# A graph layer on one core: positions written out, counts in fixed chunks, rows kept resident, nine dense tiles

## The chip, the cores and the metric

The kernel runs on one core of a Trainium2 chip. The metric is the device time of one execution in microseconds (us); a time "before" is the median of three runs. Engine names in the rows: PE is the matrix engine (PEld its weight loads), DVE the vector engine, ACT the scalar engine, POOL GpSimd, SP the engine that here only starts transfers and passes on their arrivals. A "q" behind a name (DVEq) is that engine's sequencer.

## The reference

```python
xn = layernorm(x)                                  # x is 6250 x 256, float32
h = maxk(xn @ W_neigh, 32)                         # each row keeps its 32 largest values
summed = segment_sum(h[src], dst)                  # 200000 edges, dst is sorted
neigh = summed / max(degree(dst), 1)
mix = ((q(xn) @ context) * gate(xn)) @ Wproj + bproj   # context: softmax(k) over all rows, times v
x = x + xn @ W_self + neigh + mix
y = layernorm(x)
w = y @ wr + br                                    # 3124 rows with the largest w are selected
out = x + y, and for the selected rows: + (gelu(y @ w1 + b1) @ w2 + b2) * w
```

What matters here is `summed`. The targets are drawn as 6250 times the square of a uniform number, so the first targets have by far the most edges. Every row of h is kept as two float16 halves of 256 values, so a stored row is 512 float16 values (1 KB) in `rows_d` in the chip's memory.

## The kernel before

The 6250 rows are 50 tiles of T = 125. The edges, in the order of their targets, are cut into chunks of 128 and groups of four chunks (512 edges).

Three stages follow each other. The first (to about 330 us) lays out the edges, computes h and k and v for all tiles, stores the rows of h and forms the context. The second, which is what the change touches, is a row of 50 positions, one tile each: it sums the messages of the tile and computes everything up to w. The third selects rows and runs the feed-forward part.

A tile of the second stage is summed in one of two ways.

- A sparse tile is gathered. POOL issues four indirect DMAs for a group (`gathers`, L729), each bringing 128 rows of 1 KB into a ring of 8 groups; it may refill a slot when PE has counted up `s_slot_free`. DVE makes one-hot rows of the group's targets (`visit`, L1480, four chunks in one instruction), into a ring of 8. PE does four matmuls of 512 columns (L1074) and four of 2 columns for the degrees (L1075) per visit. A tile has one visit more than it has groups, because a group on a tile's edge is visited by both.
- A dense tile (the first tiles, with the most edges) is not gathered. Its sum is a matrix of counts (target row by source row) times all rows of h. The counts are made in 13 windows of 10 target rows. For each chunk of 128 edges of a window DVE makes a one-hot of the source's place in its tile (125 wide) and one of the combined key of target and source tile (500 wide), and PE multiplies them into a bank of PSUM (L1048). ACT copies a finished window to `counts16` (L866). When all 13 are there, PE multiplies the counts by the rows of h (L1117, 50 matmuls of 512 columns) and sums the degrees (L1123).

Eight tiles are dense. The 50 positions are three hardware loops (one turn of ten positions, three turns, one turn), and the order inside a turn is fixed by tables: `SHARE` says how many windows of the coming dense tile are counted at each sparse position, `SUMMED` at which positions the eight pieces of rows (`PIECES`, reloaded from `rows_d` by ACT for every dense tile into the two halves of `hs`) are multiplied. How many chunks a window has is found from the edges while the kernel runs: DVE and PE read the window's bounds with `value_load` (L459) and loop over pairs of chunks (`keys_of` on DVE, L1499 and L1507; `count` on PE, L1048). The pairs pass through a ring of 8 pairs, guarded by `s_hot` (DVE to PE) and `s_hot_free` (PE to DVE). A position's groups are cut into up to four stretches, and the windows are counted between them.

The order of the work in position n:

- PE: wait for `s_pfree` (DVE has read the projection of n-1); load the bounds of the coming position and the windows (L459); mix_hidden for n+2 (L1015), project for n (L1032, L1035), mix_open for n+1 (L1021, L1027); possibly one piece of rows; then the opening zero matmuls (L1142, L1143); visits, windows and pieces in turn; the closing matmuls (L1152, L1153), the last of which raises `s_agg`.
- DVE: one-hots of the visits and the keys of the windows in turn; `row_chain` of position n-1 (L1542 to L1570); base_x and base_p (L1606, L1609, which raises `s_pfree`); gate_pre for n+2 (L1467); mix for n+2 (L1471); the loads of bounds for the next position; wait for `s_agg`; copy the sum out (L1616 to L1621, raising `s_deg` and `s_aggfree`).
- ACT: the small transfers of the position, the tanh of the gate, the copies of finished windows, the reloads of `hs`, the GELU, and the store of the row block.
- SP: waits for every group's landing and passes it on as `s_landed`; after every four groups it starts a transfer of the next indices (`indices`, L595), without which POOL cannot go on.

## Time and profile before

| | us |
|---|---|
| median of three runs | 2484.12 (2483.62 to 2513.19) |
| the profiled execution: its own time | 2499.61 |
| its span (first to last instruction) | 2497.5 |
| clock granted to PE, mean over the span | 0.749 of full speed |
| PE busy | 1546.7 |
| DVE busy | 1280.0 |
| POOL busy | 1129.9 |
| ACT busy | 238.0 |

The span is what the rows below are read against; the execution's own time has 2.1 us more, and stands 0.6% above the median of the runs. Busy times of the engines overlap, and none reaches two thirds of the span.

### The profile page before, as it was taken

What the parts mean: (1) busy time and instruction counts of PE and PEld (TensorE: products, weight loads), DVE (VectorE), ACT (ScalarE), POOL (GpSimd) and SP (SyncE); (2) the same over time, 40 slices, a digit from 0 to 9 for tenths busy, and PEclk for the clock granted to TensorE, in tenths of its full rate; (3) what the DMA queues carried; (4) which work ended last, traced back from release to release, by engine and by line L of the source; (5) the groups of instructions that cost most, each with busy time, mean ns of one, the idle gap of its engine ahead of it and who ended that gap; (6) DMA issues with size and microseconds to landing.
All of it is one profiled execution on the core that took longest, in us unless ns stands there. A gap on an engine that the chain in (4) does not pass through costs nothing.

```text
span 2497.5 us, 35631 instructions
## 1 busy us (share of the span) xinstructions
PE 1546.7 (62%) x7023; PEld 1006.7 (40%) x7024; DVE 1280.0 (51%) x4041; ACT 238.0 (10%) x499; POOL 1129.9 (45%) x1207
## 2 busy tenths in 40 slices
PE   1985546565646655655665565646656756662998
PEld 0542433343333433433343343434433534442566
DVE  6999436554632366356346445446355365365111
ACT  1542200000000000000000000000000000000211
POOL 1455634566656445345533543624425255431312
PEclk8997667686767677767677767867766766875999
DMA  8221422233346322722632542722723733740301
GB/s 166 67 77 54 122 63 64 85 99 93 97 119 168 99 66 83 186 62 84 163 94 71 150 113 69 183 78 73 193 58 95 161 93 98 189 98 26 87 17 27
DMA packets 175766, 249.12 MB, mean 100 GB/s; under 512 B 39962, under 2 KB 135759, under 8 KB 175650
## 3 DMA queue, kind: packets, MB, share of 16 engines
q0 software_dynamic: 55152, 135.74, 20.0%
q10 hardware_dynamic: 90492, 91.90, 14.5%
q1 hardware_dynamic: 30006, 20.05, 3.5%
q8 instruction: 59, 0.97, 0.2%
q14 instruction: 57, 0.47, 0.1%
HBM read 211.32 MB, written 35.71 MB: 99 GB/s over the span
## 4 chain that ended last, share of the span: by engine, by line
PE 29%; issue 26%; DVE 15%; DVEq 9%; another core or an unknown queue 9%; DMA 8%; ACTq 2%; SPq 1%; POOL 0%; ACT 0%; POOLq 0%
PE bank L1074 6%; PE bank L1048 6%; DMA region_k<-rows_d 5%; PE bank L1193 3%; PE bank L1207 3%; DVE region_k L1507 2%; PE bank L1117 2%; DVEq L459 2%; PE bank L1032 2%; DVEq L1518 2%; DMA gs_wide<-gs_d 2%; DVE region_r L1381 1%; PE bank L1035 1%; DMA region_k<-in_x_dram 1%
## 5 line engine op out<-in xcount | busy, mean ns | idle before, releaser
L729 POOL DMA_INDIRECT ring<-rows_d,stage x960 | 948.1, 988 | 1018.6 <-PE bank L1074 661.9
L1074 PE MATMUL bank<-ring,region_v 128*125 x1120 | 418.9, 478 | 119.1 <-issue 113.9
L1048 PE MATMUL bank<-region_k 128*125 x830 | 292.6, 461 | 171.9 <-issue 147.8
L1507 DVE TENSOR_SCALAR region_k<-iota,win_start,region_k 128x500 f16 x830 | 306.3, 408 | 26.2 <-issue 21.7
L1480 DVE SCALAR_TENSOR_TENSOR region_v<-iota,tile_start,dstT 128x500 f16 x280 | 206.1, 739 | 181.1 <-issue 156.0
L1074 PEld LDWEIGHTS bank<-ring,region_v 128*125 x1120 | 178.1, 159 | 250.7 <-issue 195.8
L1499 DVE SCALAR_TENSOR_TENSOR region_k<-iota,region_k 128x250 f16 x415 | 173.2, 417 | 167.5 <-issue 110.7
L1616 DVE TENSOR_SCALAR col_deg<-bank 125x1 f32<-125x1 f32 x50 | 7.8, 157 | 469.7 <-remote 216.7
L1048 PEld LDWEIGHTS bank<-region_k 128*125 x830 | 115.5, 153 | 298.3 <-issue 282.8
L1015 PE MATMUL bank<-region_v,wg1g 128*64 128x125 f32 x208 | 51.9, 395 | 282.2 <-issue 262.3
L1075 PE MATMUL bank<-ones,region_v 128*125 128x2 f16 x1120 | 200.0, 179 | 7.5 <-issue 7.2
L1075 PEld LDWEIGHTS bank<-ones,region_v 128*125 x1120 | 182.5, 163 | 18.7 <-issue 16.9
L1117 PE MATMUL bank<-region_k 125*125 125x512 f16 x400 | 127.8, 467 | 90.9 <-DMA region_k<-rows_d 76.4
L1015 PEld LDWEIGHTS bank<-region_v,wg1g 128*64 128x64 f32 x208 | 33.7, 201 | 286.4 <-issue 283.1
L866 ACT ACTIVATE region_k<-bank 125x500 f16<-125x500 f32 (+1 forms) x104 | 60.1, 579 | 896.2 <-remote 532.6
L1117 PEld LDWEIGHTS bank<-region_k 125*125 125x125 f16 x400 | 60.4, 164 | 132.6 <-DMA region_k<-rows_d 83.8
L1032 PE MATMUL bank<-region_v 128*125 128x256 f32 x200 | 93.0, 609 | 5.6 <-issue 5.6
L960 PE MATMUL bank<-region_r 128*125 128x512 f32 x200 | 96.3, 604 | 0.0
L1193 PE MATMUL bank<-region_k,region_v 128*128 128x500 f32 (+1 forms) x224 | 88.2, 553 | 1.4 <-DVE region_k L1733 1.4
L1207 PE MATMUL bank<-region_v,region_k 128*125 128x256 f32 x400 | 87.3, 379 | 0.0
L753 POOL DMA_INDIRECT out_dram<-region_r,region_v x24 | 28.6, 1191 | 126.8 <-DVE region_r L1753 123.1
L1035 PE MATMUL bank<-region_v 128*125 128x256 f32 x200 | 79.6, 535 | 7.9 <-issue 7.9
(302 smaller groups left out, 1987.1 us busy)
## 6 DMA issues: line engine op xcount, KB each, us to landing
region_k<-rows_d ACTq DMA_DIRECT2D x48, 672.0 KB
ring<-rows_d,stage POOLq DMA_INDIRECT x960
kept_d<-region_v ACTq DMA_DIRECT2D x50, 252.0 KB
region_k<-rows_d ACTq DMA_DIRECT2D x16, 784.0 KB
region_v<-xT_d ACTq DMA_DIRECT2D x53, 125.0 KB
xT_d<-region_r ACTq DMA_DIRECT2D x51, 125.0 KB, 2.0
rows_d<-region_r SPq DMA_DIRECT2D x50, 125.0 KB
region_k<-in_x_dram ACTq DMA_DIRECT2D x50, 125.0 KB
```

Of the source, the lines that this page charges most:

```text
L729: pool.indirect_dma_start(out=ring[:, c, :], out_offset=None, in_=rows_d, in_offset=bass.IndirectOffsetOnAxis(ap=stage[:, c:c + 1], axis=0 ...
L1032: pe.matmul(p_sum, xTc[:, turn, k * T:(k + 1) * T], w_self[:, k, :], start=(k == 0), stop=False)
L1035: m = pe.matmul(p_sum, mixT[:, k, :], wproj[:, k, :], start=False, stop=(k == KC - 1))
L1048: m = pe.matmul(out, lo, key, start=False, stop=False, skip_group_check=True)
L1074: m = pe.matmul(total, onehot_s, row_s, start=False, stop=False, skip_group_check=True)
L1075: d = pe.matmul(deg_sum, onehot_s, ones16[:], start=False, stop=False, skip_group_check=True)
L1117: m = pe.matmul(dense_sum, counts16[:, b, :], hs[:, q % 2, (b - first) * 2 * C:(b - first + 1) * 2 * C], start=False, stop=False, skip_gro ...
L1193: m = pe.matmul(up_bank(n)[:, 0:wide], w1[:, k, n * 128:(n + 1) * 128], x3T[:, g % 2, k, 0:wide], start=(k == 0), stop=(k == KC - 1))
L1207: m = pe.matmul(y_pair(h)[:, u % 2, :], hid[:, g % 2, n, u * T:(u + 1) * T], w2[:, n, :], start=(n == 0), stop=(n == NH - 1))
L1480: dve.scalar_tensor_tensor(out=part(hot_bytes, HOT, SLOT_HOT, hot, 0, SLOT_HOT).bitcast(F16).rearrange("p (a t) -> p a t", a=GC), in0=iota ...
L1499: dve.scalar_tensor_tensor(out=part(pair_bytes, HOT_PAIRS, SLOT_PAIR, slot, 0, KEYS_AT).bitcast(F16) .rearrange("p (a t) -> p a t", a=PAIR ...
L1507: last = dve.tensor_scalar(part(pair_bytes, HOT_PAIRS, SLOT_PAIR, slot, KEYS_AT + u * KEYS * 2, KEYS * 2).bitcast(F16), iota[:, 0:KEYS], p ...
```

## The change

The change does eight things in the second stage.

1. The three hardware loops go. The 50 positions are written out, from a list `ORDER` made while the kernel is built.
2. Nine tiles are dense instead of eight.
3. A window has a fixed number of chunks, from the distribution of the targets (`window_chunks`: mean plus six roots of the mean, plus the share of a chunk that an unaligned start needs). The sum over the 117 windows is 978 chunks. If a window's edges didn't fit, the general path (everything gathered) would be taken.
4. The windows are cut into 126 units of at most 16 chunks. ACT loads a window's first chunk (one `value_load` for each window) and copies the source places and the keys of a unit to a small buffer at a fixed place, adding the window's start on the way (`stage`). DVE makes two one-hots for a chunk with two `tensor_scalar` instructions at fixed addresses; the ring holds 16 chunks, and PE frees it chunk by chunk. PE's count is one matmul for a chunk; the zero matmuls around a window go (the first and last matmul carry start and stop).
5. In a position, PE does all groups in one stretch, closes the sum and raises `s_agg`, and only then counts the position's units. DVE makes the one-hots of all visits, then `row_chain` of n-1, then the units' keys, then base_x and the rest as before.
6. All rows of h (6.4 MB) are loaded once by SP into `table`, after the context is done; a dense tile is then 50 pairs of matmuls (512 columns and 2 columns) at its own position. The reloads of `hs` and the pieces go.
7. DVE and PE load bounds only for the groups of sparse tiles.
8. In the first stage POOL fills the tables with some 110 small iotas and memsets instead of about ten, and DVE's short chain that makes the bounds is changed in a few steps.

By the build-time list, the sparse tiles 9 to 16 come first with 267 chunks counted beside them, then dense tile 0; then four sparse positions before each of the dense tiles 1 to 4, three before 5, four before 6 and 7, three before 8; the last three sparse tiles have no counts.

```diff
-    TURNS_OF = (1, 3, 1)
-    DENSE_AT = (9, 4, 6)
-    PAIR = 2
-    HOT_PAIRS = 8
-    SHARE = ((2, 2, 2, 2, 2, 2, 1, 0, 0, 0), (4, 4, 5, 0, 0), (4, 3, 3, 3, 0, 0, 0, 0, 0, 0))
+    ND = 9
+    COUNT_HOT = 16
+    UNIT = 16
+    STAGED = 8
+    def window_chunks(w):
+        low, high = (w // NW * T + min(w % NW * WIN + wide, T) for wide in (0, WIN))
+        mean = E * (math.sqrt(high / N) - math.sqrt(low / N))
+        return math.ceil((mean + 6 * math.sqrt(mean) + CHUNK - 1) / CHUNK)
...
         def positions(engine, position):
-            for loop in range(len(TURNS_OF)):
-                with engine.Fori(0, TURNS_OF[loop]) as i:
-                    for s in range(PER):
-                        position(Place(loop, i, s))
+            for n in range(NT):
+                position(Place(n))
...
         @block.sync
+            sp.wait_ge(s_xpad, 32)
+            sp.wait_ge(s_ctx, 2)
+            spread(sp, table, rows_t, s_table)
             passes = load(sp, T_PASSES, 1, BLOCKS[0][1])
             ...
             landings(0, passes)
...
         @block.scalar
-            def load_h(q): ...
+            def stage(unit):
+                if unit.first:
+                    windows[unit.window] = load(act, T_WIN + unit.window, 0, CH - CAPACITY[unit.window])
+                if unit.number >= STAGED:
+                    act.wait_ge(s_hot, UNITS[unit.number - STAGED].at + UNITS[unit.number - STAGED].chunks)
+                at = windows[unit.window] + unit.offset
+                act.activation(lo_staged[:, unit.number % STAGED, 0:unit.chunks], src_lo[:, bass.ds(at, unit.chunks)], ACT.Copy)
+                act.activation(key_staged[:, unit.number % STAGED, 0:unit.chunks], keys[:, bass.ds(at, unit.chunks)], ACT.Identity,
+                               bias=starts[:, unit.window:unit.window + 1]).then_inc(s_staged, 1)
...
         @block.tensor
-            def count_window(d, k, half):
-                def count(v):
-                    pe.wait_ge(s_hot, v)
-                    slot = pe.snap((v % HOT_PAIRS) * SLOT_PAIR)
-                    for u in range(PAIR):
-                        ...
-                        m = pe.matmul(out, lo, key, start=False, stop=False, skip_group_check=True)
-                    m.then_inc(s_hot_free, 1)
-                ...
-                with pe.Fori(cuts[-2], cuts[-1]) as v:
-                    count(v)
+            def count(unit):
+                out = count_bank(unit.window)
+                if unit.first and unit.window >= 2:
+                    pe.wait_ge(s_evac, unit.window - 1)
+                for c in range(unit.at, unit.at + unit.chunks):
+                    lo, key = hot_slot(c)
+                    pe.wait_ge(s_hot, c + 1)
+                    m = pe.matmul(out, lo, key, start=(c == WINDOW_AT[unit.window]), stop=(c + 1 == WINDOW_AT[unit.window + 1]))
+                    m.then_inc(s_counts if c + 1 == WINDOW_AT[unit.window + 1] else s_hot_free, 1)
...
             def position(at_):
-                    cuts = cut(pe, g0, g1, len(parts) + len(sums))
-                    for first, end, counted, rows in zip(...):
-                        with pe.If(end > first):
-                            with pe.Fori(first, end) as g:
-                                visit(finals, g, True, total)
-                        for part_of in counted:
-                            count_window(d, *part_of)
-                        for q in rows:
-                            from_rows(q)
+                def gathered(g0, g1, finals):
+                    with pe.If(g1 > g0):
+                        with pe.Fori(g0, g1) as g:
+                            visit(finals, g, True, total)
                     visit(finals, g1, False, total)
...
                 if not at_.dense:
-                    gathered(True)
+                    gathered(*mine)
                 else:
+                    pe.wait_ge(s_evac, (at_.tile + 1) * NW)
+                    pe.wait_ge(s_table, 32)
                     with pe.If(dense > 0):
-                        degrees_from_counts()
-                    from_rows(summed[r][-1])
+                        for b in range(NT):
+                            pe.matmul(total, counts16[:, b, :], table[:, b, :], start=False, stop=False, skip_group_check=True)
+                            pe.matmul(deg_sum, counts16[:, b, :], ones16[0:T, :], start=False, stop=False, skip_group_check=True)
                 ...
                 pe.matmul(deg_sum, ..., stop=True, ...).then_inc(s_agg, 1)
+                for unit in at_.units:
+                    count(unit)
...
         @block.vector
-            def window(d, k, half):
-                def keys_of(v):
-                    dve.wait_ge(s_hot_free, v)
-                    dve.scalar_tensor_tensor(out=<2 chunks x 125>, in0=iota, scalar=0.0, in1=src_lo of 2 chunks, ...)
-                    for u in range(PAIR):
-                        last = dve.tensor_scalar(<key, 500>, iota[:, 0:KEYS], win_start, keys of the chunk, ALU.add, ALU.is_equal)
-                    last.then_inc(s_hot, 1)
-                ...
-                with dve.Fori(cuts[-2], cuts[-1]) as v:
-                    keys_of(v)
+            def count(unit):
+                dve.wait_ge(s_staged, unit.number + 1)
+                for u in range(unit.chunks):
+                    c, at = unit.at + u, unit.number % STAGED
+                    lo, key = hot_slot(c)
+                    if c >= COUNT_HOT:
+                        free(c - COUNT_HOT)
+                    dve.tensor_scalar(lo, iota[:, 0:T], lo_staged[:, at, u:u + 1], None, ALU.is_equal)
+                    dve.tensor_scalar(key, iota[:, 0:KEYS], key_staged[:, at, u:u + 1], None, ALU.is_equal).then_inc(s_hot, 1)
...
                 before = at_.before()
                 if before is not None:
                     row_chain(before)
+                for unit in at_.units:
+                    count(unit)
...
                 ends.look_ahead(at_)
-                if not at_.last:
-                    spans.look(at_.after(1))
                 dve.wait_ge(s_agg, one)
```

## Rows read from the trace of the kernel before

**Rows 1.** Windows: busy us (count) by engine, granted PE clock, DMA share, GB/s.

```profile
0.00:330.00 330.00, 197.74 (x791) 126.27 (x792) 251.96 (x807) 101.97 (x237) 153.66 (x228) 0.84 0.37 94
330.00:842.00 512.00, 297.28 (x1324) 182.53 (x1324) 248.15 (x704) 14.98 (x33) 296.61 (x300) 0.70 0.37 102
842.00:2235.00 1393.00, 854.75 (x4154) 560.55 (x4154) 706.08 (x2145) 82.56 (x170) 617.52 (x628) 0.73 0.43 111
2235.00:2498.00 263.00, 196.97 (x756) 137.32 (x756) 73.81 (x386) 38.54 (x59) 62.12 (x51) 0.84 0.16 41
```

**Rows 2.** Groups by line, 330 to 2190 us: busy, mean ns, idle before and releasers.

```profile
L729 POOL DMA_INDIRECT ring<-rows_d,stage x904 | 889.2, 984 | 975.4 <-PE bank L1074 641.1 <-issue 249.6 <-remote 84.7
L1074 PE MATMUL bank<-ring,region_v 128*125 x1060 | 398.1, 479 | 113.9 <-issue 108.7 <-DVE region_v L1480 3.2 <-SPq L602 0.5
L1507 DVE TENSOR_SCALAR region_k<-iota,win_start,region_k 128x500 f16 x830 | 306.3, 408 | 26.2 <-issue 21.7 <-remote 2.9 <-PE bank L1048 1.0
L1048 PE MATMUL bank<-region_k 128*125 x830 | 292.6, 461 | 171.9 <-issue 147.8 <-DVE region_k L1507 18.3
L1480 DVE SCALAR_TENSOR_TENSOR region_v<-iota,tile_start,dstT 128x500 f16 x265 | 195.1, 739 | 175.2 <-issue 150.8 <-remote 16.2 <-PE bank L1075 0.5
L1499 DVE SCALAR_TENSOR_TENSOR region_k<-iota,region_k 128x250 f16 x415 | 173.2, 417 | 167.5 <-issue 110.7 <-remote 33.9 <-PE bank L1048 21.9
L1117 PE MATMUL bank<-region_k 125*125 125x512 f16 x400 | 127.8, 467 | 90.9 <-DMA region_k<-rows_d 76.4 <-issue 14.6
L1015 PE MATMUL bank<-region_v,wg1g 128*64 128x125 f32 x192 | 48.0, 395 | 277.3 <-issue 262.3 <-remote 8.4 <-DVE region_v L1471 3.8
```

**Rows 3.** Timeline of PE: where positions begin (start, us, count, idle before).

```profile
1727.63 1.09 PE L1015 MATMUL bank<-region_v,wg1g 128*64 128x125 f32 x4 [11.99 <-issue]
1761.09 0.64 PE L1015 MATMUL bank<-region_v,wg1g 128*64 128x125 f32 x4
1800.17 0.64 PE L1015 MATMUL bank<-region_v,wg1g 128*64 128x125 f32 x4 [0.77 <-issue]
1822.09 1.09 PE L1015 MATMUL bank<-region_v,wg1g 128*64 128x125 f32 x4 [8.67 <-issue]
2187.47 1.06 PE L1015 MATMUL bank<-region_v,wg1g 128*64 128x125 f32 x4 [1.88 <-DVE region_v L1471]
2192.91 0.17 PE L1142 MATMUL bank<-zeros 128*125 128x2 f16 x1
2202.72 1.07 PE L1015 MATMUL bank<-region_v,wg1g 128*64 128x125 f32 x4 [3.94 <-DVE region_v L1471]
```

**Rows 4.** One source line, value_load: ns min/median/max, first and last start.

```profile
L459 PEldq TENSOR_LOAD <-bounds x182: 4/303/2789, 298.3 to 2202.0; - x182
```

**Rows 5.** Timelines of DVE and POOL, 338 to 380 us.

```profile
338.12 1.03 POOL L729 DMA_INDIRECT ring<-rows_d,stage  x1 [28.19 <-PE bank L1074]
352.02 0.42 DVE L1499 SCALAR_TENSOR_TENSOR region_k<-iota,region_k 128x250 f16 x1 [6.60 <-issue]
363.41 0.42 DVE L1499 SCALAR_TENSOR_TENSOR region_k<-iota,region_k 128x250 f16 x1 [4.65 <-issue]
368.10 0.95 POOL L729 DMA_INDIRECT ring<-rows_d,stage  x1 [0.30 <-issue]
379.77 1.06 POOL L729 DMA_INDIRECT ring<-rows_d,stage  x1 [10.72 <-PE bank L1074]
```

**Rows 6.** Timeline of DVE: a position's row chain begins, its mix ends.

```profile
1710.31 0.47 DVE L1542 SCALAR_TENSOR_TENSOR region_v<-region_k,col_rdeg 125x256 f32<-125x256 f32 x1
1716.88 0.40 DVE L1471 SCALAR_TENSOR_TENSOR region_v<-region_v,bank 128x250 f32<-128x250 f32 x1
```

**Rows 7.** One source line: a 125-wide tensor_scalar on float16, ns min/median/max.

```profile
L1722 DVE TENSOR_SCALAR region_k<-iota,region_v x50: 244/248/2331, 2285.9 to 2295.9; 125x125 f16<-125x125 f16 x50
```

**Rows 8.** The page's DMA queues: packets, MB, share of 16 engines' span.

```profile
q10 hardware_dynamic: 90492, 91.90, 14.5%
```

**Rows 9.** Groups of POOL by line, 0 to 330 us, columns as in rows 2.

```profile
L688 POOL IOTA region_r<- 1x50 f32 (+6 forms) x10 | 1.6, 188 | 0.0
```

461 lines of the change are left out of this document (189 added, 272 removed).

## The prediction

> **What bounds the kernel now.** I read the time by stage first, then what PE waits for in the stage that the change touches, then single positions, then the other engines where PE stands still. The windows show three stages [rows 1]: 330 us of preparation, 1905 us of positions (512 for the first ten, 1393 for the rest), 263 us of selection and feed-forward. Only the middle one changes. In it PE is busy 297 + 855 = 1152 us of 1905, DVE 954, POOL 914, so no engine is the bound by its work. About 750 us are time in which PE has nothing.
>
> The groups say where they lie [rows 2]. Before L1015, the first matmul of a position, PE is idle 277 us; before the count matmuls (L1048) 172; before the gathered matmuls (L1074) 114; before the rows matmuls (L1117) 91, of it 76 for the reloads of rows. Those are 654 of the 750. Most of it carries the name "issue": no other engine is late, the sequencer itself is. The timeline tells the first kind apart [rows 3]. The position that begins at 1727.63, with five windows' bounds to load, waits 12 us; the ones at 1761.09 and 1800.17, with no windows to load, wait 0 and 0.8. A value_load has a median of 0.3 us but goes up to 2.8 [rows 4]; with its register work and its assertion it costs about 2 us there.
>
> The long ones have a place. POOL issues gathers back to back from 338.12 to 368.10; some seven us into that stream DVE's loop over pairs begins to stand still, 6.6 us before the pair at 352.02 and 4.7 us before the one at 363.41, although by the trace PE had used up the pairs that it waits for; POOL then waits until 379.77 [rows 5]. So a gather stream that has run for some ten us makes the counting exchange between DVE and PE very slow, and DVE's idle time of 168 us before L1499 is mostly this [rows 2]. POOL is no bound either: it is idle 641 us for PE to free its ring [rows 2].
>
> **Part by part.** Order of sums: the span, then the execution's own time (2.1 us more), then the median (0.6% less).
>
> *Gathers.* With nine dense tiles some 900 chunks remain; in whole rounds of 32 that is 928 indirect DMAs against 960. At (889 + 250) / 904 = 1.26 us each [rows 2] this is 40 us of POOL, which now waits for PE anyway. Nothing on the path except in the first eight positions, below.
>
> *Count of chunks.* 978 fixed ones against 830 now: 148 more, at PE's 292.6 / 830 = 0.35 us [rows 2] 52 us of PE. I drew the reference's inputs and counted: its windows touch 778 chunks and none exceeds its capacity, so the general path is not taken.
>
> *DVE's price of a chunk.* Now (306.3 + 173.2) / 830 = 0.58 us of busy time plus the loop [rows 2]. After: a 125-wide one-scalar instruction, of which 49 start within 7.7 us at the end of this kernel, 0.16 us each (50 starts in 10.0 us less the one of 2.3) [rows 7], and a 500-wide one, between that 0.16 and the present 0.37 (306.3 / 830). I take 0.27, nearer to the present form but with one scalar from memory less: 0.43 a chunk, ends 0.32 and 0.53. The Trainium skill (VectorE: DVE Perf Modes, Mode 4×_2P) gives four 16-bit results a cycle at 0.96 GHz; 375 more elements would then be 0.10 us and an estimated chunk 0.42 us, 10 us less over 978 chunks; no row here shows the one-scalar form at 500 elements.
>
> *A counted position.* With g groups, v = g + 1 visits and c chunks. DVE: copy-out and one load 1.7 us (an estimate: some four instructions like those of [rows 6] and a short load of [rows 4]; ends 1 and 4), v one-hots at (195.1 + 175.2) / 265 = 1.40 [rows 2], chain to mix 1717.28 - 1710.31 = 7.0 [rows 6], c at 0.43. PE: 2192.91 - 2187.47 = 5.4 of mixing [rows 3], v at (398.1 + 113.9) / 265 = 1.93 [rows 2], c at 0.35, 1.5 until DVE's tail releases it. POOL: 4g at 1.26. By the list:
> tiles 9 to 16, eight positions (g 7.8, c 33): DVE 35, PE 36, POOL 39;
> the next sixteen (g 5.75, c 26): 29, 29, 29;
> the next fourteen (g 4.5, c 21): 25.5, 25, 23.
> The largest of each, 8 x 39 + 16 x 29.4 + 14 x 25.5 = 1140 us, is the floor. Moving the counts behind the sum's close puts DVE's chain ahead of its keys, but PE is in its visits then; what is queued behind the counts on DVE is base_p, mix and the copy-out, for which PE's next position waits. That is why the two paths add nearly whole and why the three engines meet.
>
> *What the streams add.* The visits now stand together, so a position's gathers are one stream of 23 to 39 us instead of two or three shorter ones, and the counts fall into its old part. For it: no loops, no register work, and the first 16 of a position's chunks need no signal of PE's, since they fit the ring. Lower end 0. Upper end: DVE gets its 17th slot only as the stream ends, and a position lasts 5.4 + 2 + the stream + 3 + 1.5, that is 51, 41 and 35 us, 1554 in all. I take the positions at 50, 35 and 29 (first ones near their POOL bound and with the longest streams, later ones near the floor): 400 + 560 + 406 = 1366.
>
> *The rest of the stage.* Three positions without counts at 2202.72 - 2187.47 = 15 us [rows 3]: 45. Nine dense ones: a dense position takes 1822.09 - 1800.17 = 22 us now, with two pieces and the degrees [rows 3]; after, all 50 pairs lie in it, 12.5 times the four pairs of a visit at 398.1 / 265 = 1.5 us [rows 2] or 19 us, with 5.4 of mixing and 1 of closing, and they wait for nothing (the 76 us of L1117's DMA waits go). Ends 20 and 32, I take 26: 234. The table: 6250 packets of 1 KB at 14.5% x 2497.5 x 16 / 90492 = 0.064 us on 16 engines are 25 us [rows 8]; SP can start it only when the context is done, shortly before 330, and the index transfers that POOL needs from 338.12 on [rows 5] are queued behind it on SP. The ring's eight groups cover 8 visits of the first position, so of some 10 us of lateness most shows: 12, ends 0 and 30, paid once.
>
> *The start.* POOL's 100 more small instructions at 0.19 [rows 9] are 19 us. POOL is busy 154 of the first 330 us [rows 1], and these stand at its beginning, while the edges are still being loaded; DVE asks for the tables only with its bounds. Ends 0 and 19, I take 0. DVE's own chain loses as many steps as it gains. ACT's 117 loads and 252 small activations stand beside PE's mixing and visits: at 3 units and three loads of up to 2.8 us it is ready when DVE's chain ends (about 18 us into the position). Zero; if that cover fails, 3 us for each of 38 positions.
>
> *Sum.* 1366 + 45 + 234 + 12 = 1657 against 1905: 248 us less. Span 2250, own time 2252, median 2252 x 2484 / 2500 = 2238.
>
> **The rivals.**
> *Clean.* The static exchange isn't touched by the streams. For it: in the trace straight-line stretches (the chain of [rows 6] stood inside a stream) keep their pace; against it, PE's signals seemed to reach DVE late in [rows 5], and those stay. Then 1140 + 45 + 9 x 22 = 1383: 522 us less, median about 1966. The Trainium skill (Runtime: NRT & Kernel Launch, Instruction fetch mechanics) says that taken branches break the prefetch of instructions and straight code does not; by that rule this is the outcome, and the waits in loops alone of [rows 5] agree with it.
> *Paced by the stream.* The upper end above: 1554 + 45 + 234 + 25 = 1858, 47 less, median about 2437. The loads and reloads saved come back as waits for the ring of count slots.
> *Blocked, the slower side.* If no release at all reaches DVE while the stream runs, the work behind the 17th chunk follows serially: stream 39, 29 or 23, then 3, (c - 16) x 0.43 and the rest of PE's counts and mixing, 62, 48 and 40 us a position: 1824 + 45 + 234 + 25 = 2128, 223 more, median about 2705. It decides at once c is over 16 and the signals are later than some 15 us; [rows 5] shows single ones of 7.
> *The change does not do what it says* (general path): excluded by the count.
>
> **How the numbers follow.** Forecast 0.50, clean 0.17, paced 0.18, blocked 0.10, others 0.05. Predicted: 2238, given as 2240. The forecast's own bounds: chunk price -110 to +100 (978 x 0.1), dense +-50, table -12 to +18, so some 2110 to 2370. To leave out 2 in 10 the range cuts half of the clean case and the blocked one: 2060 to 2450. A change under 2% (2434 to 2534) can hardly be told from none here. Faster by more: 0.50 + 0.17 + half of paced + 0.01 = 0.77; within 2%: 0.11; slower: 0.12.
>
> **What would show it.** Right: idle before the first matmul of a position near 1 to 3 us; no DMA wait at the dense matmuls; 928 gathers; the 500-wide instruction near 0.27 us apart; counted positions of 50, 35 and 29 us; PE's granted clock above 0.75 in the stage. Wrong: DVE idle before its 125-wide one-hots in the second half of units (paced or blocked); ACT's staging the last to come before a count; a first position that stands more than 30 us for its ninth group; count positions of 40 us with small chunk counts.

## The result, and the profile after

The changed kernel took 2408.9 us (median of four, 2395.5 to 2427.6) beside 2483.9 for the kernel before on the same chip: a ratio of 0.968, with an interval of 0.957 to 0.978. It is 75 us faster, where 244 were forecast. The profiled execution has a span of 2397.4 us.

Later runs met two kinds of chip, and the account needs both. On the prediction's chip and on two of the later ones the kernel before took 2484 to 2520 us; I call them the **first kind**. On three others it took 2107 to 2113, the **second kind**. (The record doesn't number the prediction's chip, and each chip of the first kind was met in one sitting only, so "kind" may be a condition that a chip was in as well as a property of it.) On the second kind the changed kernel took 1882.1 us beside 2109.5: a ratio of 0.892 (0.889 to 0.895), 227 us less.

The windows of the changed kernel on the prediction's chip, columns as in [rows 1]:

```profile
0.00:330.00 330.00, 199.71 (x805) 127.54 (x806) 253.20 (x814) 102.73 (x243) 158.91 (x313) 0.84 0.40 100
330.00:842.00 512.00, 277.09 (x1255) 160.01 (x1254) 233.98 (x838) 23.05 (x78) 265.29 (x269) 0.69 0.33 89
842.00:2140.00 1298.00, 829.17 (x4183) 520.84 (x4181) 742.05 (x2725) 124.28 (x385) 627.30 (x628) 0.77 0.30 85
2140.00:2398.00 258.00, 195.72 (x754) 137.00 (x754) 70.64 (x374) 38.11 (x58) 62.02 (x51) 0.85 0.15 41
```

Only the positions changed, as forecast: 1810 us where they were 1905. PE's work in them fell by 46 us, from 1152 to 1106. The rest of its time is idle still, 704 us where it was 753. The groups of the same stretch, 330 to 2140, say what became of it:

```profile
L722 POOL DMA_INDIRECT ring<-rows_d,stage x896 | 892.6, 996 | 931.5 <-PE bank L1052 577.8 <-issue 260.3 <-DMA stage<-srcT 47.4
L1039 PE MATMUL bank<-region_k 128*125 128x500 f16 x978 | 400.0, 505 | 524.1 <-ACT region_k L869 185.6 <-issue 183.4 <-DVE region_k L1457 135.2
L1457 DVE TENSOR_SCALAR region_k<-iota,region_k 128x500 f16<-128x500 f16 x978 | 352.8, 361 | 12.6 <-issue 12.3
L1052 PE MATMUL bank<-ring,region_v 128*125 x1084 | 327.9, 427 | 59.4 <-issue 36.0 <-SPq L585 23.3
L1456 DVE TENSOR_SCALAR region_k<-iota,region_k 128x125 f16<-128x125 f16 x978 | 281.9, 288 | 517.1 <-remote 414.9 <-PE bank L1039 61.8 <-issue 31.8
L1099 PE MATMUL bank<-region_r,region_k 125*125 125x512 f16 x450 | 140.9, 442 | 14.0 <-issue 14.0
L1008 PE MATMUL bank<-region_v,wg1g 128*64 128x125 f32 x196 | 40.7, 344 | 32.8 <-DVE region_v L1431 17.4 <-issue 14.3 <-DVE region_v L1427 1.2
```

Set them beside [rows 2]. PE's idle time before a position's first matmul (L1008, was L1015) fell from 277 to 33 us, that before the dense matmuls from 91 to 14, that before the gathered ones from 114 to 59. Before the count matmuls (L1039, was L1048) it rose from 172 to 524. The four come to 654 before and 630 after. So the three waits that the change was to take away have shrunk by 376 us, and 352 came back before the count matmuls. DVE, which feeds those, stands idle 517 us before its 125-wide one-hots, 415 of them marked "remote", where the profile finds nothing on this core that released it just then.

Position 11 shows how that looks. DVE's timeline (start, us, idle before in brackets) while POOL issues a gather each 1.25 us, from 940.7 to 970.6:

```profile
958.11 0.26 DVE L1456 TENSOR_SCALAR region_k<-iota,region_k 128x125 f16<-128x125 f16 x1 [0.21 <-PE bank L1039]
958.28 0.34 DVE L1457 TENSOR_SCALAR region_k<-iota,region_k 128x500 f16<-128x500 f16 x1
960.13 0.26 DVE L1456 TENSOR_SCALAR region_k<-iota,region_k 128x125 f16<-128x125 f16 x1 [1.50 <-remote]
960.30 0.34 DVE L1457 TENSOR_SCALAR region_k<-iota,region_k 128x500 f16<-128x500 f16 x1
...
962.26 0.49 DVE L1456 TENSOR_SCALAR region_k<-iota,region_k 128x125 f16<-128x125 f16 x1 [0.67 <-remote]
...
964.36 0.26 DVE L1456 TENSOR_SCALAR region_k<-iota,region_k 128x125 f16<-128x125 f16 x1 [1.47 <-remote]
...
966.47 0.26 DVE L1456 TENSOR_SCALAR region_k<-iota,region_k 128x125 f16<-128x125 f16 x1 [1.60 <-remote]
...
974.87 0.26 DVE L1456 TENSOR_SCALAR region_k<-iota,region_k 128x125 f16<-128x125 f16 x1 [0.90 <-PE bank L1039]
```

and PE's timeline of the same time:

```profile
957.18 1.45 PE L1039 MATMUL bank<-region_k 128*125 128x500 f16 x2 [0.60 <-issue]
967.11 3.18 PE L1039 MATMUL bank<-region_k 128*125 128x500 f16 x7 [8.48 <-issue]
971.93 0.42 PE L1039 MATMUL bank<-region_k 128*125 128x500 f16 x1 [1.64 <-issue]
```

A pair of one-hots takes DVE 0.43 us; here it starts one each 0.7 to 2.1 us. The slots that it waits for had been used up long before: the pair at 960.13 waits for the slot of the sixteenth chunk back. PE ended that one at 949.4 us, and the trace records the arrival of its increment at 960.11. The recorded arrivals of s_hot_free lie 0.7, 1.4 or 2.1 us apart until the last gathers have landed, and then 14 come within 0.5 us, from 974.88 on, 0.03 us apart. PE's own wait of 8.5 us before 967.11 is the same thing by another way: it waits for ACT to empty a bank, and ACT for the word that the window was complete, which PE had given at 951.1 (the tenth chunk of the position closes it) and which is recorded at 966.45, 15 us later.

From 300 us to the end, 750 of the 1673 recorded arrivals of PE's increments are late, which here means that no matmul with that increment ended within 0.2 us of them. In the same kernel on a chip of the second kind it is 13 of 1779. In the kernel before it is 507 of 1285 on the first kind and 14 of 1399 on the second.

### The profile page after: what moved, and what is told of

Same layout as the page of the kernel before. It is cut to its first block, busy times and chain, and to the rows that moved or that the text cites. A ratio compares the mean times of both kernels' runs of the same rounds, so it can differ in the third digit from the quotient of the medians.

```text
span 2397.4 us, 29660 instructions
## 1 busy us (share of the span) xinstructions
PE 1501.7 (63%) x6995; PEld 945.4 (39%) x6995; DVE 1299.9 (54%) x4748; ACT 288.2 (12%) x764; POOL 1113.5 (46%) x1260
## 3 DMA queue, kind: packets, MB, share of 16 engines
q0 software_dynamic: 53616, 131.54, 19.3%
## 4 chain that ended last, share of the span: by engine, by line
another core or an unknown queue 28%; PE 28%; DVE 20%; issue 14%; ACTq 3%; DVEq 2%; ACT 2%; SPq 2%; DMA 0%; POOL 0%; POOLq 0%
PE bank L1099 6%; DVE region_k L1457 5%; DVE region_k L1456 4%; PE bank L1039 4%; PE bank L1146 4%; PE bank L1160 3%; PE bank L1052 3%; PE bank L953 1%; ACTq L461 1%; DVE region_r L1341 1%; PE bank L1025 1%; SPq L530 1%; DVE region_r L1337 1%; ACT region_k L869 1%
## 5 line engine op out<-in xcount | busy, mean ns | idle before, releaser
L1039 PE MATMUL bank<-region_k 128*125 128x500 f16 x978 | 400.0, 505 | 524.1 <-ACT region_k L869 185.6
L1456 DVE TENSOR_SCALAR region_k<-iota,region_k 128x125 f16<-128x125 f16 x978 | 281.9, 288 | 517.1 <-remote 414.9
L1039 PEld LDWEIGHTS bank<-region_k 128*125 128x125 f16 x978 | 155.1, 166 | 751.8 <-issue 316.5
L1052 PE MATMUL bank<-ring,region_v 128*125 x1084 | 327.9, 427 | 59.4 <-issue 36.0
L1457 DVE TENSOR_SCALAR region_k<-iota,region_k 128x500 f16<-128x500 f16 x978 | 352.8, 361 | 12.6 <-issue 12.3
L1052 PEld LDWEIGHTS bank<-ring,region_v 128*125 x1084 | 154.4, 142 | 150.3 <-issue 75.1
L1053 PE MATMUL bank<-ones,region_v 128*125 128x2 f16 x1084 | 184.2, 170 | 20.8 <-issue 20.3
L1053 PEld LDWEIGHTS bank<-ones,region_v 128*125 x1084 | 156.8, 145 | 28.5 <-issue 28.5
L1099 PE MATMUL bank<-region_r,region_k 125*125 125x512 f16 x450 | 140.9, 442 | 14.0 <-issue 14.0
L1099 PEld LDWEIGHTS bank<-region_r,region_k 125*125 125x125 f16 x450 | 67.0, 149 | 54.5 <-issue 24.7
L1100 PE MATMUL bank<-ones,region_k 125*125 125x2 f16 x450 | 77.6, 172 | 6.9 <-issue 6.6
L1160 PEld LDWEIGHTS bank<-region_v,region_k 128*125 128x125 f32 x400 | 74.7, 188 | 10.9
L1025 PE MATMUL bank<-region_v 128*125 128x256 f32 x200 | 74.3, 506 | 0.0
```

The source lines that it names most:

```text
L1025: pe.matmul(p_sum, xTc[:, turn, k * T:(k + 1) * T], w_self[:, k, :], start=(k == 0), stop=False)
L1039: m = pe.matmul(out, lo, key, start=(c == WINDOW_AT[unit.window]), stop=(c + 1 == WINDOW_AT[unit.window + 1]))
L1052: m = pe.matmul(total, onehot_s, row_s, start=False, stop=False, skip_group_check=True)
L1053: d = pe.matmul(deg_sum, onehot_s, ones16[:], start=False, stop=False, skip_group_check=True)
L1099: pe.matmul(total, counts16[:, b, :], table[:, b, :], start=False, stop=False, skip_group_check=True)
L1160: m = pe.matmul(y_pair(h)[:, u % 2, :], hid[:, g % 2, n, u * T:(u + 1) * T], w2[:, n, :], start=(n == 0), stop=(n == NH - 1))
```

## The experiments

The theories by their letters: A, each increment of PE's takes its turn on the way while gathers stream, so their number counts. B, the work itself is slower beside the gathers. C, each increment is late by a fixed time. D, traffic on the DMA engines and the memory makes them late. E, which came up on the way, each matmul takes its turn, with an increment or without.

Every kernel is an edit of the changed one. Positions are quoted as five numbers: the first, the mean of the next seven, of the next sixteen counted, of the last fourteen counted, and of the nine dense ones. For the changed kernel they are 119.6, 52.8, 39.2, 29.3, 26.6 on the prediction's chip (with 17.4 for each of the last three).

**Releases in lumps of four, then of eight** (four in the edit below).

```
-  m.then_inc(s_counts if last_of_window else s_hot_free, 1)
+  if last_of_window: m.then_inc(s_counts, 1)
+  elif c % LUMP == LUMP - 1: m.then_inc(s_hot_free, 1)
-  if c >= COUNT_HOT: free(c - COUNT_HOT)
+  if c >= COUNT_HOT and c % LUMP == 0: free(c - COUNT_HOT + LUMP - 1)
```

> PE signals freed count slots once for four chunks (the last of each four, and each window's last as now); DVE waits once for four slots. Nothing is left out. Theory A (late releases): in the changed kernel the records of PE's increments of s_hot_free arrive one by one, 0.7 to 2.1 us apart, while POOL issues gathers, and in a burst 34 ns apart when it stops; DVE starts its next one-hot 0.02 us after each arrival. If the number of increments is what is slow, four chunks for one arrival take 4 x 0.43 us of DVE's work against some 2 us, and the wait nearly goes: counted positions (now 52.8, 39.2 and 29.3 us in the three groups) near their POOL and DVE bounds of 42, 33 and 27, so 100 to 200 us less than the changed kernel, 2210 to 2310. Theory B (the work itself is slower beside the gathers: memory contention or clock): lumps change nothing, 2409 within 15. Theory C (an increment is late by a fixed age whatever their number): coarser lumps only hold slots longer, 10 to 40 us slower.

> As the run with lumps of four, with eight chunks to a release: the ring is two halves. Nothing is left out. Theory A: 100 to 200 us less than the changed kernel, within 30 us of the lumps of four on either side (half as many increments, but the halves overlap less: DVE needs 8 x 0.43 = 3.4 us for a half, and an arrival every 2 to 3 us would cover it). Theory B: no change. Theory C: slower by 20 to 60 us, more than with lumps of four.

They landed on a chip of the second kind: 1884.2 us, a ratio of 0.894 (0.893 to 0.896), and 1892.4, 0.899 (0.897 to 0.901), beside 0.892 for the changed kernel itself (below). Lumps of four change nothing and lumps of eight lose 10 us: there were no late releases there to cure. They say nothing of the first kind.

**The table later.**

```
-  spread(sp, table, rows_t, s_table)
+  if 1 <= n <= 5: act.dma_start(table[:, part, :], rows_t[:, part, :]).then_inc(s_table, 16)
```

> The table of rows is loaded by ACT in five parts in positions 1 to 5 instead of by SP ahead of its first landings. Nothing is left out. In the changed kernel SP's second table instruction lasts 19.6 us (318.8 to 338.4), PE's first visit waits 8.2 us for SP's word of a landing, and the next index transfers, queued behind the table, let POOL start only at 357.4; position 0 lasts 119.6 us. If the table's place is the cause, POOL starts near 340 and position 0 lasts 85 to 100 us: 20 to 35 us less, 2375 to 2390. Rival: position 0 is bound by its 56 gathers and by the slow releases of its 48 chunks, and stays above 108 us; ACT is held some 4 us by each part, and the whole is within 12 us of the changed kernel.

The cause, on the prediction's chip: SP's timeline, then POOL's and PE's.

```profile
318.83 19.57 SPq L530 DMA_DIRECT2D region_r<-rows_d  x1
341.75 1.51 SPq L578 DMA_DIRECT2D stage<-srcT  x2
```

```profile
309.05 0.95 POOL L722 DMA_INDIRECT ring<-rows_d,stage  x1 [0.30 <-issue]
357.41 1.07 POOL L722 DMA_INDIRECT ring<-rows_d,stage  x1 [47.41 <-DMA stage<-srcT]
```

```profile
332.85 0.20 PE L1091 MATMUL bank<-zeros 128*125 128x2 f16 x1
341.25 0.68 PE L1052 MATMUL bank<-ring,region_v 128*125 x1 [8.20 <-SPq L585]
```

The instruction holds SP for 19.6 us, so PE hears 8 us late that its rows have landed, and the indices behind it on the queue arrive 15 us after they are issued. Measured on the second kind: 1860.1 us, 0.883 (0.882 to 0.885); 22 us less than the changed kernel, the first position 69.9 in place of 93.2 and nothing else moved by over 1 us. The mechanism is shown, at 23 us. On the first kind it wasn't tried.

**A quarter of the gathers.** The loop over a group's four gathers runs once, and the landing is counted accordingly. The kernel leaves out three quarters of the gathered messages (the ring holds zeros there); the visits and counts of PE and DVE are all kept.

> Leaves out three of the four gathers of every group (the ring holds zeros there), so that a position's stream is 5 to 8 gathers, under 10 us; the visits, counts and signals of PE and DVE are all kept. Theory A (the exchange is slow only beside a running stream): chunks exchange at DVE's 0.43 us everywhere; positions near 36, 29 and 25 us, position 0 near 55, some 400 us less than the changed kernel, about 2010. Rival (the written-out exchange is slow by itself, by the fetch of its code or by its waits): positions still at 45, 35 and 27, some 100 to 200 us less, all of it from POOL's shorter work.

> The run with a quarter of the gathers once more (three of four are left out, the ring holds zeros there). Where the kernel before takes 2107 it measured 1755. Where it takes over 2400: if the stream of gathers is what makes the ends of matmuls late, the streams of 5 to 8 gathers are too short for it and it takes 1755 to 1800 here too; if that chip's exchange is slow by itself, 2100 or more.

The same kernel on both kinds: 1754.7 us where the kernel before takes 2107, and 1757.0 (one execution) where it takes 2490. Positions 61, 28.5, 25.2, 22.2, 20.3 and 64, 28.5, 25.1, 22.3, 19.9. The first expectation was made for the first kind, about 2010 by theory A and 2209 to 2309 by its rival; 1757 lies some 250 us below even the lower, since it left POOL's bound out only in part. The second named 1755 to 1800 if the stream is the cause, and met it. The groups on the chip of the first kind, 330 to 1500:

```profile
L1459 DVE TENSOR_SCALAR region_k<-iota,region_k 128x500 f16<-128x500 f16 x978 | 338.8, 346 | 0.0
L1458 DVE TENSOR_SCALAR region_k<-iota,region_k 128x125 f16<-128x125 f16 x978 | 256.2, 262 | 23.5 <-PE bank L1041 14.2 <-DVE region_v L1514 6.3 <-issue 3.0
L723 POOL DMA_INDIRECT ring<-rows_d,stage x224 | 228.3, 1019 | 975.0 <-PE bank L1054 848.1 <-DMA stage<-srcT 56.8 <-issue 45.4
```

DVE's idle time before its one-hots is 24 us in place of 517. This is the strongest result of the study: without long streams the two kinds of chip are equal within 3 us, so the 527 us between the changed kernel's two times (2409 and 1882) come from what a long stream does on one of them, and neither from the written-out exchange nor from an engine that is slower whatever runs beside it. (On the first kind 207 of 1735 arrivals come late even here; little waits for them.)

**The changed kernel and the kernel before, unaltered, on the second kind.**

> The changed kernel itself, unaltered, beside the others: the chip of the first four runs ran the kernel before in 2107 us where the one of the prediction took 2484, and the changed kernel has no time of its own on it. Where the kernel before takes 2107: theory A, that the releases are late only on the other chip (in the run with a later table here no increment of PE's was late by more than a few tenths in streams of over 40 us), puts it at 1880 to 1900, beside the lumps of four. If lumps of four helped here too, it would be 1950 or more. Where the kernel before takes 2484: 2409 within 20.

> The kernel before, unaltered, for its trace on a chip other than that of the prediction. Where it takes 2107 us in place of 2484: theory A says that the 377 us between the two are waits for late increments of PE's: DVE's idle time before its counting one-hots (168 us on the other chip) and PE's before a position's first matmul (277 us) mostly gone, the busy time of the same instructions within 5%. Rival: the other chip is slower in its work (clock, memory), and the busy times carry the difference.

1882.1 us and 2106.3. The changed kernel's positions are 93.2, 39.5, 26.4, 22.4, 19.3, and 15.6 for each of the last three. Its groups, 330 to 1625:

```profile
L722 POOL DMA_INDIRECT ring<-rows_d,stage x896 | 943.7, 1053 | 365.6 <-issue 262.2 <-PE bank L1052 76.9 <-DMA stage<-srcT 26.5
L1457 DVE TENSOR_SCALAR region_k<-iota,region_k 128x500 f16<-128x500 f16 x978 | 356.5, 365 | 0.0
L1039 PE MATMUL bank<-region_k 128*125 128x500 f16 x978 | 355.8, 435 | 41.7 <-DVE region_k L1457 23.9
L1052 PE MATMUL bank<-ring,region_v 128*125 x1065 | 342.4, 444 | 143.2 <-SPq L585 142.7 <-issue 0.5
L1456 DVE TENSOR_SCALAR region_k<-iota,region_k 128x125 f16<-128x125 f16 x978 | 295.1, 302 | 132.1 <-PE bank L1039 122.8 <-DVE region_v L1512 9.3
L1099 PE MATMUL bank<-region_r,region_k 125*125 125x512 f16 x450 | 124.6, 409 | 0.0
```

The page of the same profile, over the whole span, has the first matmul of a position:

```profile
L1008 PE MATMUL bank<-region_v,wg1g 128*64 128x125 f32 x208 | 38.2, 314 | 62.2 <-DVE region_v L1431 35.0
```

and these are the groups of the kernel before on such a chip, as the page of its profile has them:

```profile
L729 POOL DMA_INDIRECT ring<-rows_d,stage x960 | 970.3, 1011 | 611.8 <-PE bank L1074 332.5
L1048 PE MATMUL bank<-region_k 128*125 x830 | 251.3, 408 | 26.8 <-DVE region_k L1507 7.9
L1015 PE MATMUL bank<-region_v,wg1g 128*64 128x125 f32 x208 | 50.0, 387 | 265.0 <-issue 232.7
L1117 PE MATMUL bank<-region_k 125*125 125x512 f16 x400 | 126.3, 463 | 95.4 <-DMA region_k<-rows_d 95.2
L1499 DVE SCALAR_TENSOR_TENSOR region_k<-iota,region_k 128x250 f16 x415 | 172.3, 415 | 12.1 <-PE bank L1048 10.8
```

DVE's wait before the counting one-hots is 12 us in place of the 168 of [rows 2], at the same busy time per instruction (415 ns against 417); PE's before its first matmul is 265 us, hardly less than the 277 (282 over the whole span). So the expectation was right in its first half and wrong in its second: the loads' price is there on both kinds, the late releases on one. And there the change does what it was forecast to do: 265 to 62 us before the first matmul, 95 to 0 before the dense ones, and 42 us before the counts in place of 27. What PE mostly waits for there after the change is the gathered rows, 143 us before L1052 for SP's word that they have landed.

**Counts first.** The count loops moved ahead of the groups on PE and DVE again.

> The second part of the change undone: a position's counts come ahead of its groups and of its sum's close on PE, and ahead of the groups on DVE; all else is as in the changed kernel. Where releases are late in an old stream, the counts now meet the young part of it and the visits wait for rows that have landed long before; the two effects are each some 5 us a position, so within 60 us of the changed kernel on that chip. Where they are prompt: POOL's ring is refilled only after the counts, so a position gives POOL its slots later by 10 to 14 us; in the first eight, which are bound by POOL, up to 10 us each, and none elsewhere: 40 to 120 us slower than the changed kernel. Rival: the order is worth nothing, within 15 us.

> The second part of the change undone, as in the earlier run of that kernel, which took 1994 beside 1882. Where the kernel before takes over 2400: the first 16 chunks need no release and the next meet a stream that is young, so a count of 25 to 30 chunks takes 15 us in place of 25 to 30; the visits then wait late for PE's slots of one-hots instead. If the order decides where lateness is paid, 60 to 200 us faster than the changed kernel's 2409; if the stream only moves with the order (POOL starts on a position's slots as PE frees them, and the wait for its end is the same), within 60 us of it; if POOL's later refill decides as on the other chips, 50 to 120 us slower.

Both landed on chips of the second kind: 1994.4 us, 0.944 (0.939 to 0.949), and 1984.8, 0.943 (0.937 to 0.949), 103 to 112 us slower than the changed kernel. Positions 76.0, 45.7, 29.6, 24.8: 6 us more in the seven, and against the expectation 3.2 and 2.4 in the others too. POOL gets its slots later everywhere, not only where it is the bound. What the order is worth on the first kind stays open.

**More signals.**

```
+  if s < GC - 1: m.then_inc(s_more, 1); d.then_inc(s_more, 1)
```

> Adds increments of a semaphore that nobody reads: the six matmuls of a visit that had none each give one, 1626 more of PE's increments. Nothing is left out. If PE's increments are carried one by one, in order, at a rate that a stream of gathers lowers to one in 2 to 3 us (theory A), these stand ahead of the counts' releases and the counts' exchange begins some 48 increments later: on a chip that shows late releases 10 us or more on each of 41 positions, 400 us slower; on one that doesn't, no change (within 10 us). If only single increments are late (theory C), no change on either.

Second kind again: 1884.4 us, 0.892 (0.889 to 0.895), no change. It says only that increments are free there.

**Both at once, and fewer chunks.** The capacity of a window is its mean plus one standard deviation instead of six.

```
-  return math.ceil((mean + 6 * math.sqrt(mean) + CHUNK - 1) / CHUNK)
+  return math.ceil((mean + 1 * math.sqrt(mean) + CHUNK - 1) / CHUNK)
```

> The later table and the lumps of four together. Nothing is left out. The later table alone measured 1860 beside 1884 for lumps alone on the chip where the kernel before takes 2107: there the sum is 1860 within 10, since PE's releases are not late. On a chip where the kernel before takes 2484, theory A gives 100 to 200 us for the lumps and 20 to 35 for the table: 2180 to 2290.

> The later table, and the windows' capacities with one standard deviation to spare in place of six: 865 fixed chunks instead of 978. These inputs still fit. Nothing is left out. Where the kernel before takes 2107: positions past the eighth are bound by DVE, on whose line a chunk costs 0.43 to 0.46 us; of the 113 chunks 82 lie there, 35 us less than the later table's 1860: about 1825. In the first eight, bound by the gathers, nothing. Rival (POOL or PE binds throughout): less than 10 us. Where it takes 2484: a chunk beyond the sixteenth costs an arrival of 2 us, some 100 us less than the later table alone there.

> The same with releases of four slots. Where the kernel before takes 2107: the same time as without them within 5 us. Where it takes 2484: theory A gives 80 to 180 us less than without them, theory B nothing.

> The later table and 865 chunks instead of 978, which took 1835 where the kernel before takes 2107. Nothing is left out. Where it takes over 2400: the table 20 us, and the 82 to 113 chunks fewer at 1.4 to 2.1 us each where they are paced by arrivals, less what the stream's end gives back anyway: 60 to 170 us less than 2409, 2240 to 2350. If positions end with their stream whatever the chunks: 2370 to 2400.

Second kind in all: 1862.0 us, 0.882 (0.879 to 0.884); 1835.2, 0.869 (0.865 to 0.873); 1836.3, 0.869 (0.866 to 0.873); 1832.4, 0.869 (0.866 to 0.872). Lumps change nothing. The 113 chunks are worth 25 to 28 us, 0.22 to 0.25 each or 0.3 for those past the eighth position; 35 were expected. So part of a chunk's 0.43 us of DVE lies on the path and part doesn't. The version with the later table and 865 chunks beats both kernels: 47 to 50 us less than the changed one, 275 less than the one before. It has more windows that a different draw could overfill, which then takes the general path.

**Copies beside it.** Of 1 MB in DRAM, issued by SP with every second group that lands.

```
+  hold(sp, s_copied[q // 2], (j + 1) * 16)
+  sp.dma_start(copy_d[q // 2], rows_d[0:1024]...).then_inc(s_copied[q // 2], 16)
```

> The changed kernel, and beside it SP copies 1 MB from the rows in DRAM to a scratch tensor in DRAM with every second group that lands: 116 MB read and 116 MB written more during the positions. Nothing is left out. Where the kernel before takes 2107: if late releases come from traffic on the DMA engines and the memory (theory D), DVE's waits before its 125-wide one-hots appear in the late part of each stream, and the time goes from 1882 to 2100 or more. Rival (they belong to the other chip): gathers and loads are somewhat slower, the exchange keeps its 0.43 us a chunk, the time stays under 1960. Where the kernel before takes 2484: 2409 or more under both.

> The same copies, with releases of four slots. Where the traffic made releases late: theory A gives back most of what it cost in the exchange, 100 us or more; where it didn't, the time of the copies with single releases within 10 us. Where the kernel before takes 2484: 100 to 200 us less than with single releases by theory A, the same by theory B.

Both on a chip of the first kind: 2428.8 us, 0.962 (0.940 to 0.983), and 2437.7, 0.965 (0.951 to 0.980). The changed kernel's ratio is 0.968. The copies raised what the DMA moved from 200 to 321 MB and cost nothing that can be measured, so there is no sign of theory D on this kind of chip; on the other, where it would have shown best, it wasn't tried. And lumps of four gained nothing, where theory A wanted 100 us. DVE's timeline in the kernel with both:

```profile
930.13 0.34 DVE L1471 TENSOR_SCALAR region_k<-iota,region_k 128x500 f16<-128x500 f16 x1
943.43 0.26 DVE L1470 TENSOR_SCALAR region_k<-iota,region_k 128x125 f16<-128x125 f16 x1 [12.96 <-remote]
...
944.99 0.34 DVE L1471 TENSOR_SCALAR region_k<-iota,region_k 128x500 f16<-128x500 f16 x1
951.14 0.26 DVE L1470 TENSOR_SCALAR region_k<-iota,region_k 128x125 f16<-128x125 f16 x1 [5.82 <-remote]
```

Four pairs in a row, then a wait: one release comes in 7.7 us for four chunks, as long as four single ones at 1.4 to 2.1. Theory A falls, as far as lumps beside the copies can tell: the number of increments is not what counts. Theory C, a fixed lateness, falls as well: the visits' signals, given 1.1 us apart, are recorded 2.7, 4.4, 6.4 and 7.8 us apart. Theory B falls for DVE: its one-hots take 288 and 361 ns in the changed kernel on the first kind, 302 and 365 on the second. For PE the equal times of the quartered gathers speak against a slower engine, but only without the stream. The profile models the ends of matmuls, so the traces can't tell a matmul that really ends late beside a stream from one whose signal alone is late. What is left of the theories is E, in either reading.

**More matmuls, and fewer.**

```
+  pe.matmul(deg_sum, zeros16[:, 0:T], zeros16[:, 0:2], start=False, stop=False, ...)
```

```
-  d = pe.matmul(deg_sum, onehot_s, ones16[:], ...)
+  if s == GC - 1: d = pe.matmul(deg_sum, onehot_s, ones16[:], ...)
```

> Four matmuls of zeros on two columns more in every visit (twelve in place of eight), with no increment of their own; their sum is unchanged and nothing is left out. Theory E (beside an old stream of gathers the ends of PE's matmuls, each of them, reach the semaphores in order and one by one, 0.7 us or more apart): the first release of a count slot stands 32 matmuls further back in a position of eight visits, so 20 us or more later, until the stream ends: where the kernel before takes over 2400, 150 to 400 us slower than the changed kernel's 2409. Where it takes 2107: only PE's own 0.05 us for each of the 1084, in positions bound by POOL or DVE: 0 to 50 us slower than 1882. Theory A (increments alone count): no more than 50 us slower on either.

> Leaves out the degree's matmul in three of a visit's four chunks (five matmuls in place of eight), so that the degrees come out as those of one chunk in four; increments are as they were. Theory E: 24 matmuls fewer ahead of the first release in a position of eight visits; where the kernel before takes over 2400, counted positions come down by 5 to 12 us each, 150 to 350 us faster than 2409. Where it takes 2107: 0 to 30 us faster than 1882. Theory A: within 40 us of the changed kernel on either.

The second leaves out three quarters of the gathered tiles' degrees. Both on the first kind: 2421.9 us, 0.971 (0.956 to 0.985), and 2337.2, 0.937 (0.926 to 0.947). The totals don't bear theory E out. 32 matmuls more to a position cost nothing that can be measured, where theory E wanted 150 us at least and theory A allowed 50. 24 fewer gain 72 us against 2409 (77 by the ratios to the kernel before, whose intervals don't meet), more than theory A's 40 and half of theory E's least. The records of arrivals say more. The median time between the recorded arrivals of two visits' signals (s_oh_free), 12 to 18 us into a stream:

```
matmuls in a visit    median us between arrivals    cases
 12 (four empty)            9.6                       18
  8 (changed kernel)        6.8                       16
  5 (fewer)                 5.7                        9
```

PE issues a visit in 1.1 us, or 1.3 with the empty ones. So a signal seems to wait for the matmuls around it, 0.8 to 1.1 us for each of these; later in a stream a count's matmul takes 1.4 to 2.1. Two things weaken the table. The spacing doesn't follow the number of matmuls in proportion: from 12 to 8 it falls by 2.8 us, from 8 to 5 by 1.1. And records are missing on this kind of chip: of 271 visits' arrivals the traces have 251, 238 and 215 (on the second kind all 271), and a gap over a missing one counts double. In positions with none missing the medians are 8.6 (15 cases) and 6.4 (5 cases) for 12 and 8 matmuls; for 5 there is no case. In the kernel with empty matmuls the visits themselves come to wait for slots, with 91 us idle before L1052 in place of 59, and PE's idle time before the counts falls from 524 to 340: the lateness moved. That is also why the totals hardly answer. Whatever is held back is let go when the stream ends, so such a position ends 10 to 13 us after its last gather, however long the queue was: in positions 9, 14 and 24 of the changed kernel the last gather started 43.6, 35.8 and 30.4 us in, and they lasted 55.3, 48.8 and 40.2. That PE's signals are late and come in order is shown by the arrivals. That every matmul takes a turn, with an increment or without, is the reading that fits the arrivals best; the totals don't confirm it, and it is not shown.

## Why the prediction was right and wrong

**Direction, place and range held.** The kernel is faster by over 2%, only the positions changed, and 2409 lies between 2060 and 2450. It is nearest to the rival that I called paced by the stream (2437), and 169 us above my forecast. The size of the gain did not hold: 75 us where 244 were forecast.

**The step that failed** is "What the streams add" of the part on the positions, for the prediction's chip. I had seen in [rows 5] that the exchange between DVE and PE gets slow some ten us into a stream. I took the loops for half of the reason ("For it: no loops, no register work") and put positions at 50, 35 and 29 us, between the floor and the stream's pace (51, 41 and 35). Written out, the exchange has no loops and is just as slow: the seven after the first measured 52.8, the sixteen 39.2, the fourteen 29.3. Against the forecast that is 20, 67 and 4 us in all. The upper end, and not the middle, was right for the first two. What makes it slow is that PE's signals arrive late, as the arrivals and the quartered gathers show, and the written-out code, which has no loops there, waits all the same. On the second kind, where the signals are prompt, the same code took 39.5, 26.4 and 22.4 us, so the lateness costs 13, 13 and 7 us a position, where my forecast had 11, 6 and 3.5 over the floor.

**The table.** I took 12 us (0 to 30), for SP's queue. The delay measured is 23 us on the second kind, within the bounds, and the mechanism is as I put it: the indices behind the table, and SP late with its landings. But the first position was 58 us over its 50 + 12, nearly as much as the sixteen. Three things make that up. I gave it the mean of the first eight (7.8 groups), but it has 14: with the table out of the way it took 69.9 us on the second kind, 20 over its 50. The table cost 11 more than its 12. The remaining 26 or so (119.6 against 93.2) are what the first kind adds, where its 48 chunks lie in a long stream.

**The rest of the sum.** Dense positions took 26.6 us on the mean (forecast 26) on the first kind, and that is luck: four take 18 to 22, as a position with no waits should, and five take 30 to 34. The one that begins at 1008.36 stands 8.0 us before L1020, for ACT's part of the gate, and its first dense matmul starts 14 us in. On the second kind all nine take 18 to 21. There is no DMA wait at the dense matmuls. The last three 52 in all (45). 928 gathers. The 500-wide instruction follows after 0.26 us and a chunk takes DVE 0.43 (forecast 0.27 and 0.43). The start cost nothing. PE's granted clock in the later positions is 0.77, above the 0.75 that I named, but 0.69 in the first ones, as before. ACT's staging is not among what ends DVE's waits; what ACT does hold up is a count's start: its emptying of a bank ends 186 us of PE's wait, itself late by the same signals. The 161 us between 1657 and the measured 1819 are 58 + 20 + 67 + 4 for the counted positions, 5 for the dense and 7 for the last.

**On chips of the second kind** the sum's floor is met, but for the first position (93.2 us): 39.5, 26.4 and 22.4 us beside 39, 29.4 and 25.5, dense positions 19.3 beside the clean case's 22. The clean rival describes these chips, and its 522 us didn't come only because the kernel before doesn't pay for late releases there either; the gain is 227. The forecast of 248 came out near that by luck: for these chips the kernel before stands over 370 us too high in it (2484 for 2110) and the changed kernel's positions 331 (1657 for 1326), and the two cancel.

**The rivals.** "Blocked", the slower side, needed no release at all to arrive in a stream; they arrive, slowly, and it didn't happen. The rule that the clean case drew on, from the Trainium skill (Runtime: NRT & Kernel Launch, Instruction fetch mechanics), is about taken branches to code outside the two pages that an engine holds. Read as widely as I read it, it would have freed written-out code of these waits; the rows of position 11 show straight code that stands 1.5 us before a pair, released within 0.02 us of an arrival, so the wait is for a signal and not for code. The loads of [rows 3] and [rows 4] did go with the code.

## What to carry to other kernels

A wait isn't the loop's just because it is seen in a loop: look up when the signal waited for was given and when it arrived, before costing its removal. Where several waits lie side by side in front of a bound that none of them touches (here the end of a gather stream), taking away one gives its time to the next, so add up idle time by engine before and after, not by line. And measure the kernel before on more than one chip: a gain of 227 us on one was 75 on another.

## What the runs showed of the hardware

The same kernel before took 2107 to 2113 us on three chips, and 2484 to 2520 on the prediction's and two others, with DVE and POOL busy within 2% of the same time (1280 and 1260 us, 1130 and 1152), PE busy 8% longer at a lower granted clock in the later positions (0.73 and 0.79), and, with a quarter of the gathers, the same time within 3 us.

On chips of the first kind, beside a stream of back-to-back indirect gathers, PE's increments arrive late and in order. In the changed kernel the first late arrival is recorded 2.7 to 8.6 us into 37 of 42 streams (median 4.3). From then on the increments of the counts come 0.7 us or a multiple of it apart, and those of visits, given 1.1 us apart, come 2 to 3 us apart at first, 5 to 8 after some 10 us and 11 to 15 after some 25. All that were held back arrive 0.03 us apart, 2 to 4 us after the last gather. Matmuls that increment nothing seem to take their turn too, which isn't shown. DVE's signals to PE and ACT's to PE showed no such delay in the stretch read above (a one-hot that ended at 955.68 released a matmul at 955.73, and ACT's emptying of a bank, which ended at 967.06, one at 967.11). On chips of the second kind the signals of visits arrived at the 1.1 us at which they were given, and 13 of 1779 arrivals were late. What makes the difference between the chips stays open, and so does what in a stream of gathers does it, POOL's issuing or the transfers; 121 MB of copies more, issued by SP, didn't add to it.

An SP transfer of 6250 rows of 1 KB in two instructions held SP's queue for 19.6 us with the second of them; the same rows in five parts from ACT cost no measurable time.
